# Waits on transfers and sums in GpSimd's scatters and gathers of a graph network kernel

## The reference

```python
xn = _layernorm(x, axis=-1)
x = x + _L0_gnn_ref(xn, edge_index, edge_weight, ...) + _L0_mix_ref(xn[None], ...)[0]
x = x + _L0_ffn_ref(_layernorm(x, axis=-1)[None], ...)[0]     # 8 experts, 2 chosen, one shared
xn = _layernorm(x, axis=-1)
x = x + _L1_gnn_ref(xn, edge_index, edge_attr_2, ...) + _L1_mix_ref(xn[None], ...)[0]
x = x + _L1_ffn_ref(_layernorm(x, axis=-1)[None], ..., L1_ffn_edge_index)[0]
```

## Time and profile before

| | us |
|---|---|
| median of 3 runs | 2920.31 |
| lowest, highest | 2916.86, 2930.26 |
| the profiled execution | 2916.22 |
| its span | 2914.4 |
| GpSimd busy | 2021.0 (69%) |
| TensorE busy | 2159.4 (74%) |
| VectorE busy | 1680.6 (58%) |
| ScalarE busy | 1184.9 (41%) |

### The profile page before, as it was taken

How to read it: one execution, slowest core, us unless ns; L and a number is a source line. 1 busy time by engine, 2 the same in 40 slices (tenths; PEclk the granted TensorE clock), 3 DMA queues, 4 the chain that set the end, 5 groups by cost and what they waited for, 6 DMA issues and landing times. The chain is left out here.

```text
span 2914.4 us, 34544 instructions
## 1 busy us (share of the span) xinstructions
PE 2159.4 (74%) x9997; PEld 1671.4 (57%) x9997; DVE 1680.6 (58%) x4678; ACT 1184.9 (41%) x3151; POOL 2021.0 (69%) x2060
## 2 busy tenths in 40 slices
PE   0275482277666768999999997788877766899993
PEld 0055361144344437878888876455555545688883
DVE  8937889366679885110010026788887767333337
ACT  0111353155555542222222213799954444244442
POOL 4777777677777766777777633777777772777761
PEclk9996555588888887999999999899988876899996
DMA  2020000533333341366666633222222251211111
GB/s 65 2 63 2 6 3 2 193 105 105 106 105 102 103 96 37 118 176 196 199 191 193 194 104 103 51 54 53 54 51 52 53 47 9 55 36 35 18 19 46
DMA packets 173390, 233.34 MB, mean 80 GB/s; under 512 B 59819, under 2 KB 136622, under 8 KB 172206
## 3 DMA queue, kind: packets, MB, share of 16 engines
q0 software_dynamic: 73664, 103.00, 15.8%
q1 hardware_dynamic: 96888, 118.21, 13.1%
q10 hardware_dynamic: 2678, 10.29, 0.9%
HBM read 192.31 MB, written 39.04 MB: 79 GB/s over the span
## 5 line engine op out<-in xcount | busy, mean ns | idle before, releaser
L831 POOL DMA_INDIRECT slots_gnn<-rec_gnn,slot_row_gnn x782 | 770.6, 985 | 285.6 <-issue 229.6
L2359 POOL DMA_INDIRECT arena<-table,rec_gnn x440 | 456.0, 1036 | 162.0 <-issue 127.7
L1222 POOL DMA_INDIRECT rows_gnn<-support,xT x416 | 401.1, 964 | 132.6 <-issue 110.9
L1266 PE MATMUL banks<-rows_gnn,one_hot 128*128 128x256 f32 x832 | 301.0, 481 | 200.4 <-DMA rows_gnn<-support,xT 175.6
L1266 PEld LDWEIGHTS banks<-rows_gnn,one_hot 128*128 128x128 f32 x832 | 162.7, 227 | 319.6 <-DMA rows_gnn<-support,xT 180.4
L2931 POOL DMA_INDIRECT source_rows<-table_g,source_router x256 | 243.1, 950 | 78.0 <-issue 65.5
L2457 PE MATMUL banks<-weighted,one_hot 128*128 128x260 f32 x880 | 266.8, 456 | 2.6 <-DVE weighted L2554 1.9
L1871 ACT ACTIVATE hidden_private<-banks,b_private 128x256 f32<-128x256 f32 x256 | 107.3, 470 | 354.7 <-PE banks L1829 354.7
L1829 PE MATMUL banks<-slot_xT,w_private 128*128 128x256 f32 x1024 | 228.4, 381 | 1.7 <-DVE slot_xT L1885 1.7
L1841 PE MATMUL banks<-w_private,hidden_private 128*128 128x256 f32 x1024 | 226.1, 379 | 0.0
L2457 PEld LDWEIGHTS banks<-weighted,one_hot 128*128 128x128 f32 x880 | 186.9, 222 | 60.1 <-issue 26.7
(11 more groups left out here) (558 smaller groups left out, 3959.2 us busy)
## 6 DMA issues: line engine op xcount, KB each, us to landing
w_private<-in_w1p SPq DMA_DIRECT2D x32, 1024.0 KB
w_private<-in_w2p SPq DMA_DIRECT2D x32, 1024.0 KB
slots_gnn<-rec_gnn,slot_row_gnn POOLq DMA_INDIRECT x782, 2.1
slot_x<-zero_rows ACTq DMA_DIRECT2D x8, 1024.0 KB, 11.2
slot_rows<-slot_x SPq DMA_DIRECT2D x32, 256.0 KB, 7.4
slot_y<-slot_out SPq DMA_DIRECT2D x32, 256.0 KB, 2.2
arena<-table,rec_gnn POOLq DMA_INDIRECT x440
rows_gnn<-support,xT POOLq DMA_INDIRECT x416, 2.7
```

The lines of the kernel that those rows point to most:

```text
L831: pool.indirect_dma_start(e.slots, bass.IndirectOffsetOnAxis(e.rows[:, j:j + 1], 0), e.rec[:, j, :], None)\
L1222: pool.indirect_dma_start(e.rows_in[:, k, :], None, table, bass.IndirectOffsetOnAxis(row, 0))\
L1266: mm = pe.matmul(bank_of(k // per), hot[:, k, :], e.rows_in[:, row, :], start=k % per == 0, stop=k % per == per - 1)
L2359: pool.indirect_dma_start(c.raw[:, t % RAW_RING, :], None, c.table1, bass.IndirectOffsetOnAxis(row, 0))\
```

## The change

It adds five waits of three kinds to GpSimd's stream.

- `scatter_records` (now for `e0` alone): at every sixteenth transfer GpSimd waits for all four quarters, that is, until every transfer issued so far has landed.
- `scatter_in_bursts` is new and does the second scatter; it counts on one semaphore and waits at every tenth transfer (BURST) until all have landed. `send_nodes0` does the same. The first part of the second scatter has 40 transfers instead of 48.
- `gather_messages` waits for `summed1` with a lead of 28 tiles (AHEAD) instead of 72, from tile 28 on. The source rows' gathers wait for `h_ready`, with FIRST_ROWS = 16 rows ahead and 16 rows for 3 units of TensorE.

```diff
+def scatter_in_bursts(c, block, ctx, e, begin, end):
+    turns = c.sem(ctx, f"scatter_turns_{e.name}_{begin}")
+    moved = c.sem(ctx, f"records_moved_{e.name}_{begin}")
+    @block.gpsimd
+    def _(pool):
+        pool.wait_ge(e.ranked, 1)
+        pool.wait_ge(e.filled, 16)
+        for j in range(begin, end):
+            if j > begin and (j - begin) % BURST == 0:
+                pool.wait_ge(moved, 16 * (j - begin))
+                pool.sem_inc(turns, 1)
+            pool.indirect_dma_start(e.slots, bass.IndirectOffsetOnAxis(e.rows[:, j:j + 1], 0), e.rec[:, j, :], None)\
+                .then_inc(moved, 16)
+        pool.wait_ge(moved, 16 * (end - begin))
@@ scatter_records
             if turn and (j - begin) % HALF == 0:
                 pool.wait_ge(moved[h], 16 * HALF * turn)
                 pool.sem_inc(turns, 1)
+            if j and j % FLIGHT == 0:
+                for part in moved:
+                    pool.wait_ge(part, 16 * HALF * turn)
+                pool.sem_inc(turns, 1)
-SCATTERED_FIRST = 48
+SCATTERED_FIRST = 40
+BURST = 10
@@ send_nodes0
+                j = t * CHOSEN + k
+                if j and j % BURST == 0:
+                    pool.wait_ge(sent, 16 * j)
+                    pool.sem_inc(turns, 1)
+AHEAD = 28
@@ gather_messages
-                if t >= RAW_RING:
-                    pool.wait_ge(c.summed1, (t - RAW_RING) // HALF + 1)
+                if t >= AHEAD:
+                    pool.wait_ge(c.summed1, (t - AHEAD) // HALF + 1)
                     pool.sem_inc(turns, 1)
+FIRST_ROWS = 16
@@ attend_stage
                 if j % HALF == 0 and turn:
                     pool.wait_ge(rows_in[h], 16 * HALF * turn)
+                    pool.sem_inc(turns, 1)
+                if j % HALF == 0 and j > FIRST_ROWS + HALF:
+                    pool.wait_ge(h_ready, FP * ((j - FIRST_ROWS) * 3 // 16))
                     pool.sem_inc(turns, 1)
@@ build
-                    scatter_records(c, block, s, e1, 0, SCATTERED_FIRST)
+                    scatter_in_bursts(c, block, s, e1, 0, SCATTERED_FIRST)
                     send_nodes0(c, block, s)
-                    scatter_records(c, block, s, e1, SCATTERED_FIRST)
+                    scatter_in_bursts(c, block, s, e1, SCATTERED_FIRST, e1.per)
```

More of the change, by code:

```diff
@@ L810, in unpack, with scatter_records @@
         ch.then(dve.tensor_copy(self.e.idx[:], self.bank[:, 0:self.e.per]))
-def scatter_records(c, block, ctx, e, begin=0, end=None):
-    end = e.per if end is None else end
+def scatter_in_bursts(c, block, ctx, e, begin, end):
[12 more added lines that the diff above has]
+        pool.wait_ge(moved, 16 * (end - begin))
+def scatter_records(c, block, ctx, e):
+    begin, end = 0, e.per
     turns = c.sem(ctx, f"scatter_turns_{e.name}_{begin}")
@@ L1674 @@
 SHARED_FIRST = 3
-SCATTERED_FIRST = 48
+SCATTERED_FIRST = 40
+BURST = 10
 def send_nodes0(c, block, ctx):
     sent = c.sem(ctx, "nodes_sent")
+    turns = c.sem(ctx, "node_turns")
     @block.gpsimd
```

## The result

The changed kernel takes 3037.4 us (median of 4 runs, 3031.5 to 3038.8) against 2923.0 (4 runs): ratio 1.0386, 95% interval 1.0357 to 1.0416. It is slower by 114 us where 100 were forecast. The span of its profiled execution is 3035.7 us against 2914.4, which is 121 us and not 114, because the profile of the kernel before is of an execution 6.8 us under its median (2916.2). Lines have moved: the first scatter is L853, the second L826, the first gathers L1244, node rows L1716, fetching L1736, message gathers L2388, source rows L2964.

The account below looks back on a forecast made before the run. GpSimd was taken to pace the first half, TensorE 1100 to 1710 us, with 49.2 us covering the second scatter. 2916.2 + 50 + 0 + 49 + 1 + 0 = 3016, with 4.1 for the median 3020 us; range 2985 to 3070.

Parts of the forecast that it names:

- Price of a drain: GpSimd's wait until its last transfer has landed: 1.92 us over the ordinary gap, 1.98 for node rows.
- Step 1: First scatter: 24 drains at 2.1 us each, nothing covers them, 50 us on the path (46 to 62).
- Step 2: Second scatter's first part and node rows: last node some 4 us later, within 15 us of cover, cost nothing.
- Step 3: Rest of second scatter: 35 drains, 88 us, fetching 56 us late after 49.2 of cover; 49 us on the path.
- The middle value of 2.5 for a drain: Rest of second scatter: 2.5 us a drain, taken between 1.92 (between loads) and 3.1 (average with loads).
- Step 4: Message gathers: the natural lead of 14 to 23 tiles meets the new wait; 1 us, bounds 0 and 5.
- step 5: Source rows' gathers: the wait on TensorE is never binding; 0 us, bounds 0 and 2.
- Rival A: Both scatters: cheap drains, every one 1.92 us because packets interleave; 74 us, time 2994; chance 0.18.
- B: Dear drains: nearly all fall into loads, or node rows and first scatter pay too; 3052 to 3080 us; chance 0.12.
- C: Faster than before: pauses relieve GpSimd and VectorE slowing one another, at most 55 us back; chance 0.04.
- D: Little change: second scatter's drains stay within its 49 us, the first is covered by something unseen; 2920 us; chance 0.04.

Follow-up runs that it names:

- x1: The kernel before with the 24 full landings in the first scatter alone; 2974.1 us, ratio 1.0187.
- y3: The kernel before with a full landing at every eighth transfer of the first scatter alone, 48 landings; 3017.0 us, ratio 1.0309.
- x3: The kernel before with 40 instead of 48 transfers ahead of the node rows and four full landings among the node rows, no others; ratio 1.0000.
- x2: The changed kernel without the first scatter's 24 landings and with the gathers' old waits; 2983.3 us, ratio 1.0210.
- y1: The changed kernel without the first scatter's landings, with the gathers' old waits and a landing at every twentieth transfer (BURST = 20); 2953.9 us, ratio 1.0093.
- y2: The changed kernel without the first scatter's landings, with the gathers' old waits and a landing at every eleventh transfer (BURST = 11); 3003.4 us, ratio 1.0278.
- x4: The kernel before with the two new waits of the gathers alone (AHEAD and FIRST_ROWS as in the change); ratio 1.0003.
- y4: The kernel before with a lead of 20 instead of 72 tiles for the message gathers, nothing else; 2958.1 us, ratio 1.0114.

## Why the prediction was right, step by step

- **Price of a drain: right in kind, too dear in size.** 1.92 us had been read from the two seams of the kernel before, where a new stage of GpSimd's stream begins; inside a scatter it is 1.76 to 1.78 in the first (gap 2.06 to 2.08) and 1.62 in the second, clear of the loads (gap 1.92). What the late landings added was larger than forecast, and the two errors nearly cancelled: that is luck.
- **Step 1, 50 us: 54.5.** Drains over their ordinary gap came to 50.6, the number forecast, but made up otherwise: 42 us at 1.77 each and 8 by three late landings, where 46 and 4 were meant. Two single pauses of 2.03 us at transfers 113 and 321, which no drain explains, make 3.5 of the difference. That nothing covers it was right (x1, y3).
- **Step 2, nothing: right** (x3), though the last node row came 9.4 us later within its stage and not 4: node rows waited for the routing as forecast (4.98 us, for VectorE), and one of the four drains fell beside the weight loads (5.03 us).
- **Step 3, 49 us: 61.6.** The path was right and one term was too small, the start of fetching, forecast 56 us late and measured 69.4 after the 56.1 of the seam before. Of these 13, the later start of the last part is 4.4. The drains were not the miss: 93.2 us less 35 gaps of 0.30 is 82.7, under the 88 forecast. The miss is three pauses at transfers 113, 226 and 339 of 6.6, 6.1 and 3.0 us, 14.8 us over the ordinary gap, which the forecast did not have; one of them here, at GpSimd:

```profile
1470.10 0.95 POOL L826 DMA_INDIRECT slots_gnn<-rec_gnn,slot_row_gnn  x1 [6.61 <-issue]
```

  They stand at the same numbers in x2, y1 and y2, and not in the kernel before or in x3. They also move the drains behind them: in the changed kernel five of the eight dear drains are those at 120, 130, 140 and at 230 and 240, 14.5 us over 1.92 each. That these would have been cheap without the pauses is not shown. From the fetch on the reckoning held: the third tile is 59 us late where 69.4 less 10 of room makes 59, and TensorE's restart cost 2.5 us against 3 (48 matmuls in 12.91 us, at a mean granted clock of 0.81).
- **The middle value of 2.5 for a drain: right for its reason, nearly by luck.** It was taken because a drain should fall back into the gap between loads. y2 shows how much hung on that: at eleven transfers a drain costs 3.33 over the ordinary gap, above the 3.1 forecast for drains spread evenly over loads and gaps, at twenty 3.08; at ten it is 2.35. The forecast had not seen that ten transfers and a drain last as long as a group of TensorE. It also had 1.92 and 0.6 for the loads where the changed kernel has 1.62 and 0.74.
- **Step 4, 1 us, and step 5, none: right** (x4); y4 shows that the margin of 23 against 24 tiles was real.
- **Rival A, 2994, fell.** The Trainium skill's rule of engines that go round packet by packet (DMA: Bandwidth & Descriptors, "Queues, rings and completion order") would have had all drains at 1.92. In the changed kernel the 8 that met the loads took 3.00 to 6.88 us. B fell, since 27 of 35 drains missed the loads; C fell by the unchanged 1013 and 958 ns; D by x1 and x2.

What stays open is the pauses. In the scatters they came only with drains, at the same transfers however many drains there were (24 or 48 in the first, where 48 had one more pause, at 217; 17, 31 or 35 in the second). In y4 they came without drains, with waits on TensorE, so a full landing is not what they need. What GpSimd waits for there the profile doesn't show (no load of instructions falls into any of the pauses of the changed kernel), and no run varied it.

## What to carry to other kernels

A wait for the transfer just issued costs its whole landing each time, and if the issuing engine sets the pace all of it is paid: count the waits, read the gap at a place where the kernel already does one, and subtract the idle time before that engine's next seam together with the room of those that wait for it (54 to 55 us here). Under other traffic ask with what period the waits meet it; here one more transfer between them cost 15 us in all instead of saving something. A limit on the lead of a gather was free as long as it lay above the lead that the pipeline takes by itself, and cost 33 us when it lay inside it.

## What the runs showed of the hardware

- A transfer of 128 records of 16 bytes that was issued alone landed in time for a gap of 1.92 to 2.08 us. In the changed kernel drains that began less than 4 us after SyncE had issued a 1 MB weight load had gaps of 3.00 to 6.88 us, those that began 4.6 us or more after it 1.91 to 2.39.
- GpSimd's stream stopped without a visible reason at transfers 113 and 321 of the first scatter (2.03 us; in y3 also 1.80 at 217), at 113, 226 and 339 of the second (3.0 to 6.8 us) and, in y4, at 113, 217 and 321 of the message gathers (1.4 to 1.5 us). In the kernel before no gap within these stages exceeds 0.31 us, and in x4, whose waits were all met, none exceeds 0.32.
- Pauses of a tenth of GpSimd's time did not change the mean duration of its scatters (1013 against 1012 ns, 958 against 958).
